# Cross-attention: the product of probabilities and values for four head pairs in a row, twice per tile, with a ring of five transposed blocks

## The reference, cut to what matters

```
x = x + xattn(layernorm(x), ctx_768)
    q, k, v = x @ Wq, context @ Wk, context @ Wv          # 16 heads of 64
    sim  = einsum('bhid,bhjd->bhij', q, k) * 64 ** -0.5
    attn = softmax(sim, axis=-1)
    out  = einsum('bhij,bhjd->bhid', attn, v)             # the product this case is about
    return out @ Wo + bo
x = x + attn(layernorm(x))
x = x + ffn(layernorm(x))
```

## Time and profile before

| | us |
|---|---|
| median of 3 runs | 2362.71 (2360.82 to 2368.18) |
| the profiled execution | 2363.8 |
| its span | 2362.0 |
| TensorE busy | 2217.5 (94%) |
| VectorE busy | 1602.8 (68%) |
| ScalarE busy | 1294.7 (55%) |
| GpSimd busy | 844.2 (36%) |

### The profile page before, as it was taken

How to read it: one execution, slowest core, us unless ns; L and a number is a source line. 1 busy time by engine, 2 the same in 40 slices (tenths; PEclk the granted TensorE clock), 3 DMA queues, 4 the chain that set the end, 5 groups by cost and what they waited for, 6 DMA issues and landing times. The chain is left out here.

```text
span 2362.0 us, 55990 instructions
## 1 busy us (share of the span) xinstructions
PE 2217.5 (94%) x18992; PEld 1996.2 (85%) x18992; DVE 1602.8 (68%) x3655; ACT 1294.7 (55%) x3906; POOL 844.2 (36%) x1022
## 2 busy tenths in 40 slices
PE   6999999999999999999995999999999966999996
PEld 5889888998889888998895999999999853888885
DVE  6666666766666666766655889898888856444442
ACT  4555555555555555555544666667666621444442
POOL 3333333333333333333332222222222222677664
PEclk9999999999999999999997999999999986999998
DMA  4000000000000000000004000000000011444334
GB/s 114 19 20 27 9 27 18 27 9 27 27 18 27 9 27 18 27 9 27 13 6 152 1 20 9 18 18 9 18 9 18 14 43 45 103 79 105 77 53 104
DMA packets 61946, 82.52 MB, mean 35 GB/s; under 512 B 9936, under 2 KB 45520, under 8 KB 61808
## 3 DMA queue, kind: packets, MB, share of 16 engines
q1 hardware_dynamic: 48912, 63.46, 8.5%
q0 software_dynamic: 12960, 18.12, 4.6%
HBM read 59.80 MB, written 25.96 MB: 36 GB/s over the span
## 5 line engine op out<-in xcount | busy, mean ns | idle before, releaser
L411 POOL TENSOR_TENSOR p_sb<-p_sb,rinv 128x512 f32<-128x512 f32 x256 | 279.2, 1090 | 809.3 <-DVE rinv L757 809.3
L669 ACT ACTIVATE p_sb<-s_ps,nmax 128x256 f32<-128x256 f32 x512 | 238.3, 470 | 186.5 <-DVE nmax L735 183.3
L735 DVE TENSOR_REDUCE nmax<-s_ps 128x2 f32<-128x512 f32 x256 | 176.8, 691 | 224.4 <-PE s_ps L65 220.3
L915 POOL TENSOR_TENSOR sp_sb<-sp_sb,srinv 128x512 f32<-128x512 f32 x128 | 133.3, 1041 | 426.1 <-DVE srinv L1109 426.1
L45 ACT CAST qk_hi<-qk_ps 128x512 fp32r<-128x512 f32 x248 | 147.0, 593 | 130.1 <-PE qk_ps L65 128.8
L1057 ACT ACTIVATE sp_sb<-sm_sb,snmax 128x128 f32<-128x128 f32 x512 | 199.3, 390 | 7.1 <-DVE snmax L1120 4.0
L754 DVE COPY pt_sb<-t_ps 128x512 f32<-128x512 f32 x256 | 176.8, 691 | 21.3 <-PE t_ps L552 7.4
L46 ACT ACTIVATE q_sb<-m_ps 64x256 fp32r<-64x256 f32 x256 | 96.9, 379 | 171.8 <-PE m_ps L65 168.0
L65 PE MATMUL qk_ps<-q_sb,wkt_hi 128*128 128x256 f32 x496 | 147.7, 320 | 26.1 <-DVE qk_hi L57 16.6
L552 PE MATMUL t_ps<-ident,p_sb 128*128 128x128 f32 x1024 | 153.5, 272 | 1.0 <-DVE pt_sb L754 1.0
L552 PEld LDWEIGHTS t_ps<-ident,p_sb 128*128 128x128 f32 x1024 | 126.5, 141 | 29.1 <-issue 1.2
(11 more groups left out here) (293 smaller groups left out, 7587.5 us busy)
## 6 DMA issues: line engine op xcount, KB each, us to landing
ctx_raw<-in_ctx_t SPq DMA_DIRECT2D x32, 256.0 KB, 2.8
ctx_raw<-in_ctx_t SPq DMA_DIRECT2D x64, 128.0 KB, 3.0
x_ring<-in_x SPq DMA_DIRECT2D x16, 256.0 KB, 2.8
x_mid<-x_ring SPq DMA_DIRECT2D x16, 256.0 KB, 2.2
xn<-f_xn SPq DMA_DIRECT2D x16, 256.0 KB, 2.2
acc<-x_sb SPq DMA_DIRECT2D x16, 256.0 KB, 2.3
e_raw<-in_gate SPq DMA_DIRECT2D x8, 512.0 KB, 3.9
e_raw<-in_up SPq DMA_DIRECT2D x8, 512.0 KB, 5.0
```

Source lines behind the costliest of these rows:

```text
L411: nc.gpsimd.tensor_tensor(prob, prob, inv, ALU.mult).then_inc(norm_done, 1)
L669: ex = nc.scalar.activation(p_sb[:, k, b * J:(b + 1) * J], s_ps[1 - w][:, b * J:(b + 1) * J], ACT.Exp, bias=nmax[:, k, b:b + 1], scale=1.0 ...
L735: nc.vector.tensor_reduce(nmax[:, (p - 1) % 4, :], s_ps[1 - w][:].rearrange("p (b j) -> p b j", b=2), AX_X, ALU.max, negate=True).then_inc ...
L915: nc.gpsimd.tensor_tensor(prob, prob, inv, ALU.mult).then_inc(norm_done, 1)
```

## The change

The product runs in steps 3 and 7 only, each time for four pairs: step 3 takes pairs 4 to 7 of the tile before, step 7 pairs 0 to 3 of the tile itself. It fills the whole bank `o_ps`, and ScalarE and VectorE split it with one 512-column instruction each. The transposed probabilities, which have to wait for up to four steps now, lie in a ring of five blocks, with a table of places (`PT_SLOT`); `Wo` is still loaded through the first four of them, so VectorE waits for its split before the first copy. The counts of the semaphores follow. In short, with unchanged lines left out:

```diff
@@ -232,7 +232,7 @@
-            pt_sb = sbuf(ph, "pt_sb", [P, 4, HALF])
+            pt_sb = sbuf(ph, "pt_sb", [P, 5, HALF])
...
+            PT_SLOT = (3, 0, 1, 2, 4, 0, 1, 2)
...
-                        if w == 1 and (not first if p < LAG_PV else cur):
+                        if p % 4 == 3 and (not first if p < LAG_PV else cur):
 
                             pe.wait_ge(t_done, n - 3)
                             pe.wait_ge(v_done, PAIRS * t + (4 if p >= LAG_PV else 0))
-                            wait(pe, ot_done, PAIRS // 2 * t + (p - 5) // 2 - 1)
-                            if first and p == LAG_PV + 1:
-                                pe.wait_ge(wk_done, PAIRS)
-                            for q in ((p - 5) % PAIRS, (p - 4) % PAIRS):
+                            wait(pe, ot_done, 2 * t - (1 if p < LAG_PV else 0))
+                            for q in range((p + 1) % PAIRS, (p + 1) % PAIRS + 4):
                                 for b in range(2):
                                     for j in range(2):
                                         k = 2 * b + j
-                                        c = (4 * ((p - 5) // 2 % 2) + 2 * (q % 2) + b) * HEAD
+                                        c = (2 * (q % 4) + b) * HEAD
                                         for h in range(2):
                                             mm = pe.matmul(o_ps[h * HEAD:(h + 1) * HEAD, c:c + HEAD],
                                                            v_sb[:, k, q * P + h * HEAD:q * P + (h + 1) * HEAD],
-                                                           pt_sb[:, q % 4, k * P + h * HEAD:k * P + (h + 1) * HEAD],
+                                                           pt_sb[:, PT_SLOT[q], k * P + h * HEAD:k * P + (h + 1) * HEAD],
                                                            start=(j == 0), stop=(j == 1))
-                            mm.then_inc(pv_mm, 2)
+                            mm.then_inc(pv_mm, 4)
...
-                            pe.wait_ge(ot_done, PAIRS // 2 * t)
+                            pe.wait_ge(ot_done, 2 * t)
...
-            def o_half(p):
-
-                c = (p - 5) // 2 % 2 * 2 * P
-                return o_ps[:, c:c + 2 * P]
-
-            def ot_part(ot, q):
-                return ot[:, q - 1:q + 1, :].rearrange("p a t -> p (a t)")
+            def ot_part(ot, p):
+                return ot[:, (p + 1) % PAIRS:(p + 1) % PAIRS + 4, :].rearrange("p a t -> p (a t)")
...
-                        if w == 1 and (not first if p < LAG_PV else cur):
+                        if p % 4 == 3 and (not first if p < LAG_PV else cur):
                             act.wait_ge(pv_mm, n - 3)
                             if p >= LAG_PV:
                                 wait(act, y_mm, t)
-                            split_hi_act(nc, ot_part(ot_hi, (p - 4) % PAIRS), o_half(p)).then_inc(ot_hi_done, 1)
+                            split_hi_act(nc, ot_part(ot_hi, p), o_ps[:]).then_inc(ot_hi_done, 1)
...
                         if (not first if p < LAG_T else cur):
                             dve.wait_ge(t_mm, n - 2)
-                            wait(dve, pv_mm, n - 6)
-                            nc.vector.tensor_copy(pt_sb[:, (p - 3) % 4, :], t_ps[:]).then_inc(t_done, 1)
+                            wait(dve, pv_mm, PAIRS * t - (0 if p >= LAG_PV else 4))
+                            if first and p == LAG_T:
+                                weights.wait_split(dve, O_SPLIT)
+                            nc.vector.tensor_copy(pt_sb[:, PT_SLOT[(p - 3) % PAIRS], :], t_ps[:]).then_inc(t_done, 1)
...
-                        if w == 1 and (not first if p < LAG_PV else cur):
-                            dve.wait_ge(ot_hi_done, PAIRS // 2 * t + (p - 3) // 2)
-                            q = (p - 4) % PAIRS
-                            split_lo_dve(nc, ot_part(ot_lo, q), o_half(p), ot_part(ot_hi, q)).then_inc(ot_done, 1)
+                        if p % 4 == 3 and (not first if p < LAG_PV else cur):
+                            dve.wait_ge(ot_hi_done, 2 * t + (1 if p >= LAG_PV else 0))
+                            split_lo_dve(nc, ot_part(ot_lo, p), o_ps[:], ot_part(ot_hi, p)).then_inc(ot_done, 1)
```

## The result

The changed kernel takes 2399.89 us (median of 4 runs, 2397.93 to 2401.5), against 2363.03 for the kernel before: ratio 1.0152, interval 1.0134 to 1.0171. It is slower by 37 us where 14 were forecast, and lies above the range. The profiled execution took 2400.78 us, its span is 2399.0.

The account below looks back on a forecast made before the run. TensorE's order was taken to bound the kernel; +14.0 us from fifteen pairs of tiles at +0.93, −0.6 in tile 31, +1.0 in the drain and 0 in tile 0 gave +14.4, so 2377 us, range 2366 to 2392.

Parts of the forecast that it names:

- What bounds the kernel: Steady stage: TensorE's order sets the time; it waits only for VectorE's split of the previous absorb, 14.3 us in all.
- The price of a block and the doubled block: Product blocks on TensorE: a step losing its block can lose 1.25 us, one whose block doubles gains 0.94.
- Odd step 1, nothing gained: Odd tiles, step 1: late absorb still starts at 618.63; gain 0 of 1.25, wait grows from 0.71 to 1.79 us.
- Steps 5, even step 1, steps 3 and 7: Gains 1.06 in each step 5, 0.58 in even step 1; losses 0.81 in odd step 3, 0.94 in the other three.
- And the granted clock: Open end: whether odd step 1's 1.79 us wait lowers TensorE's clock, as followed a 1.81 us stretch without matmuls.
- the sum: Whole kernel: +0.93 us per two tiles, fifteen times, with tile 31, the drain and tile 0; total +14.4 us.
- its rival: Clock falls after odd step 1's wait, at most 1.7 us each: 2404 in all 15 odd tiles, 2391 in half; chance 0.14.
- the row that fell after 1.81: Start of the earlier trace: 1.81 us without matmuls (29.00 to 30.81), then a stretch at clock 0.50.
- +1.0 for the drain: Drain tile: its last block of four pairs delays the output projection, +0.3 to +1.42 us, taken as +1.0.
- −0.3 for step 5 and 7 of tile 31: Tile 31 has no absorbs, so nothing waits: 2 × (0.94 − 1.25) = −0.6 us for the whole tile.
- faster: Rival: absorbs' chain gives back less and the halved seams win; at best −18 us, 2346 us; chance 0.09.
- no change: Rival: splits come up to half a microsecond sooner in steps without a block; +5 us, 2368 us; chance 0.15.

Follow-up runs that it names:

- e7_swap: Changed kernel, but in odd step 1 ScalarE copies the early absorb before the values instead of behind them; 2370.00 us (ratio to before 1.0021).
- e4_half_odd: Changed kernel, but the odd tiles keep steps 1 and 3 as before the change; 2367.84 us (ratio to before 1.0025).
- e2_fill2: Changed kernel with 2 extra matmuls of unused result in the long wait of odd step 1; 2378.31 us (ratio to before 1.0065).
- e5_fill1: Changed kernel with 1 extra matmul of unused result in the long wait of odd step 1; 2376.84 us (ratio to before 1.0046).
- e1_fill12: Changed kernel with 12 extra matmuls of unused result in the long wait of odd step 1; 2379.67 us (ratio to before 1.0061).

## Why the prediction was wrong

Point by point, by its own steps. *What bounds the kernel*: right; in every run the waits of TensorE in the steady stretch end on the absorbs' split. *The price of a block and the doubled block*: right (2.02 for 64; 2.55 from transposes to absorb). *Odd step 1, nothing gained*: right to the hundredth, and `e7_swap` showed the reason that was given, ScalarE's copy behind the values. *Steps 5, even step 1, steps 3 and 7*: right; their sum was 0.93 a round and measured 1.00, and most of the difference is the 0.04 by which each merging of steps 5 and 7 gave less. With the clock held up by one, two or twelve matmuls the changed order takes 2376.84 to 2379.67 us: the forecast of 2377 is the time of that kernel. How close it comes is in part luck: with one matmul the rounds, tiles 30 and 31 and the drain cost about 16 us more than before, and the part behind the stage, which the edit doesn't reach, took 3.4 less (1105.46 to 1102.07, from the drain's projection to the end of the span).

The step that failed is the open end "And the granted clock", which the sum counts at nothing, and the weight given to its rival: 0.14. The forecast had the wait (1.79), the row that fell after 1.81 and the words that 1.79 "lies at the row that fell", and set it aside with "that row is of the start, when matmuls were sparse around it too". The runs put 13 falls in 15 in its place. Its price was nearly right (1.52 against at most 1.7), its frequency was not (13 against "about half"), and its chance should have been the largest. The row was not a single one, either: the trace of the kernel before has a second stretch of this length at the start, and one of 2.01 near the end, both with 0.50 behind them:

```profile
42.38:44.24 1.86, 0.00 (x1) 0.03 (x1) 1.75 (x5) 1.86 (x6) 0.00 (x0) 1.00 0.81 215
...
45.25:48.66 3.41, 3.41 (x18) 3.41 (x17) 2.17 (x6) 0.92 (x2) 1.04 (x1) 0.50 0.16 46
...
2336.65:2338.66 2.01, 0.00 (x0) 0.00 (x1) 0.69 (x1) 0.89 (x2) 1.03 (x3) 1.00 0.00 0
...
2339.00:2341.00 2.00, 2.00 (x12) 2.00 (x10) 0.00 (x0) 0.00 (x0) 0.56 (x1) 0.50 0.49 53
```

Of the stretches that TensorE stood still at 1.00 in that trace, from the 29.00 of the earlier trace rows on, the longest that no fall followed took 1.40 (1992.19 to 1993.59). The rival's 13 × 1.52 = 20 us and the 14 of the sum give 34 of the 37. Smaller: from tile 31's projection to the drain's the sum had +0.7 (+1.0 for the drain, −0.3 for step 5 and 7 of tile 31), and 2.9 were measured; there the 10.1 us from 1284.20 ran at 0.50. `e4_half_odd`, with the same order from there on and a clock of 1.00, took 1.1 more than before (1235.97 to 1259.09 against 1234.58 to 1256.58), so the order was sized nearly rightly and the rest goes with the clock; this was read off and not tested by a run of its own.

The rivals "faster" and "no change" did not come: the late absorbs of steps 1, 5 and 7 start within 0.02 us of where the forecast put them. The change did what it says, and it is worth something only in steps 5 and 7, where a lost block gives 1.04 of its 1.25 back and a doubled one costs 0.94.

Not settled: why two of the 15 long waits brought no fall. Their stretches without matmuls are as long (1.79 and 1.80); the spacing of the falls speaks for their place in time, but no run tests it. The 1.9 us at the start and the 2.8 behind the stage lie within what kernels with the same order show: the first output projection starts between 95.79 (`e2_fill2`) and 99.39 (`e5_fill1`), and from the drain's projection to the end of the span it is 1102.07 (`e5_fill1`) to 1114.51 (`e1_fill12`).

## What to carry to other kernels

A piece of work that lies between two dependent steps of the engine that sets the time may be free there; moved away, it returns its wait in full and costs again at the new place. Before such a move, list for every place the earliest time at which the next instruction could start without it. Then compare the stretches that TensorE will stand still with those in the trace after which the clock fell, single long ones and shorter ones close together: where they come near one, forecast the fall, or put in a matmul that nobody needs.

## What the runs showed of the hardware that was not expected

How small a difference decides here: with 1.79 us without matmuls the clock fell in 13 of 15 tiles, with 1.67 in none of 15, with 1.55 and 1.30 in none; a single 128x256 matmul, 0.12 us of the wait, was worth 20 us. The length of one stretch is not all, though. In the changed kernel a stretch of 1.85 at the start (41.66 to 43.51) brought no fall. In the kernel before, the clock fell in the drain though none of the stretches without matmuls that the drain has ahead of the fall is longer than 1.03 us; two of 0.90 and 0.93 lie right before it (the second in the earlier trace rows):

```profile
1254.00:1256.90 2.90, 1.47 (x34) 1.33 (x35) 0.87 (x2) 0.37 (x1) 0.00 (x0) 1.00 0.00 0
1257.00:1260.30 3.30, 3.30 (x18) 3.30 (x17) 0.00 (x0) 0.00 (x0) 0.00 (x0) 0.50 0.00 0
```

The Trainium skill (TensorE: Matmul & The Clock Gate, "Why this matters for your kernels") warns of idle gaps between bursts of matmuls, but of longer ones than these; here 1.79 was enough, and in the drain several shorter ones were, and the measurement decides.
